# Two-layer graph block on one core: square root, reciprocal and shift of the normalising, once for both node groups of a step

## What is computed

```python
def conv(h, i):
    msg = h[src] * edge_weight[:, None]
    agg = jax.ops.segment_sum(msg, dst, num_segments=N)
    return agg @ W_rel[i] + b_rel[i] + h @ W_root[i]
# _layernorm: (x - m) / jnp.sqrt(v + eps), over the 128 features of a node
x = _layernorm(x + _L0_gnn_ref(x, edge_index, edge_weight, W_rel, b_rel, W_root))
x = _layernorm(x + _L1_gnn_ref(x, edge_index, edge_types, W, b))
```

## Time and profile before

| | |
|---|---|
| median of 3 runs | 1509.75 us (1504.82 to 1514.61) |
| the profiled execution | 1525.14 us, its span 1523.4 us |
| mean granted TensorE clock | 0.927 |
| busy share of the span | PE 81%, DVE 66%, POOL 55%, ACT 48% |
| layer 3, first to last residual add on DVE | 758 to 1075 us |
| last layer, first typed product to the end | 1097 to 1523 us |

### The profile page before, as it was taken

The page is one execution under the profiler, slowest core; times in us unless marked ns, Lnnn a source line. Parts: engine busy times, 40 slices in busy tenths (PEclk is TensorE's granted clock), DMA queues, the critical chain, the costliest instruction groups (busy, mean ns, idle before and its releaser), DMA issues.

```text
span 1523.4 us, 36509 instructions
## 1 busy us (share of the span) xinstructions
PE 1233.3 (81%) x6476; PEld 876.6 (58%) x6476; DVE 1000.5 (66%) x4006; ACT 729.2 (48%) x1674; POOL 831.9 (55%) x1154
## 2 busy tenths in 40 slices
PE   0599999999579997889378776778399999979984
PEld 0488888777457775667255554556145555445543
DVE  5566666565335554445289996878239999878886
ACT  0144443222124442212078886677326677756675
POOL 4776665561277775550577664650455666645520
PEclk9899999999889999999699998989669999998995
DMA  2599999999568888999599999999236666677775
GB/s 64 140 292 300 306 301 307 349 348 350 208 203 270 258 263 291 381 369 363 189 294 341 327 333 316 365 354 342 92 102 182 202 210 205 213 235 237 249 251 183
DMA packets 293061, 403.05 MB, mean 265 GB/s; under 512 B 43478, under 2 KB 202839, under 8 KB 292970
## 3 DMA queue, kind: packets, MB, share of 16 engines
q10 hardware_dynamic: 87120, 266.66, 47.3%
q1 hardware_dynamic: 180538, 83.67, 20.4%
q0 software_dynamic: 25312, 51.78, 12.8%
HBM read 222.77 MB, written 179.16 MB: 264 GB/s over the span
## 4 chain that ended last, share of the span: by engine, by line
DMA 25%; PE 24%; issue 14%; DVE 13%; SPq 13%; ACT 5%; POOL 3%; ACTq 2%; DVEq 1%; POOLq 0%
DMA win<-edge_rows 7%; PE ps_node L1256 7%; DMA feat_t<-spill 6%; PE ps_node L1247 5%; SPq L542 5%; PE ps_pair L1279 5%; DMA win<-plain_rows 4%; DVE ln_stats L1030 4%; SPq L545 3%; SPq L534 3%; DMA edge_rows<-edge_out 3%; POOL gather_ring L649 3%; PE ps_pair L1224 2%; ACT rows L1466 2%; DMA plain_rows<-gather_ring 2%
## 5 line engine op out<-in xcount | busy, mean ns | idle before, releaser
L649 POOL DMA_INDIRECT gather_ring<-h,src_ring x588 | 563.9, 959 | 261.0 <-issue 148.1
L1256 PEld LDWEIGHTS ps_node<-place,win 128*128 128x128 f32 x1764 | 288.4, 196 | 235.3 <-issue 173.7
L1256 PE MATMUL ps_node<-place,win 128*128 128x171 f32 (+1 forms) x1764 | 321.6, 319 | 68.8 <-DMA win<-plain_rows 58.9
L1412 ACT ACTIVATE next_t<-ps_node,rel_bt 128x512 f32<-128x512 f32 x294 | 199.9, 680 | 256.3 <-PE ps_node L1256 214.5
L972 DVE TENSOR_SCALAR place<-iota_row,window_node,window_weight 128x171 f32<-128x171 f32 (+1 forms) x882 | 280.6, 373 | 0.2
L1011 DVE COPY rows<-ps_pair 128x512 f32<-128x512 f32 x196 | 135.3, 690 | 210.2 <-PE ps_pair L1279 201.4
L1247 PE MATMUL ps_node<-feat_t,root_w 128*128 128x512 f32 x380 | 206.7, 627 | 58.5 <-DMA feat_t<-spill 54.7
L1466 ACT ACTIVATE rows<-resid,ln_shift,ln_rstd 128x128 f32<-128x128 f32 x576 | 235.8, 481 | 22.1 <-issue 22.1
L649 POOL DMA_INDIRECT gather_ring<-in_x,src_ring x196 | 186.7, 952 | 71.9 <-issue 55.2
L1279 PE MATMUL ps_pair<-rel_w,next_t 128*128 128x128 f32 x1568 | 208.2, 276 | 4.3 <-ACT next_t L1412 4.3
L1279 PEld LDWEIGHTS ps_pair<-rel_w,next_t 128*128 128x128 f32 x1568 | 197.6, 192 | 5.5 <-ACT next_t L1412 5.4
(11 more groups left out here) (115 smaller groups left out, 1164.0 us busy)
## 6 DMA issues: line engine op xcount, KB each, us to landing
h<-rows ACTq DMA_DIRECT2D x121, 512.0 KB
win<-plain_rows SPq DMA_DIRECT2D x588, 64.0 KB
edge_rows<-edge_out ACTq DMA_DIRECT2D x98, 264.0 KB
feat_t<-in_x_t ACTq DMA_DIRECT2D x49, 512.0 KB
plain_rows<-gather_ring ACTq DMA_DIRECT2D x98, 256.0 KB
resid<-in_x ACTq DMA_DIRECT2D x49, 512.0 KB
out_x<-rows ACTq DMA_DIRECT2D x49, 512.0 KB
spill<-next_t ACTq DMA_DIRECT2D x46, 512.0 KB
```

Of the source, the lines that this page charges most:

```text
L649: pool.indirect_dma_start(out=gather_ring[:, k.slot(4), j, 0:D], out_offset=None, in_=h_tabs[l][:, :], in_offset=bass.IndirectOffsetOnAxis ...
L1256: op = pe.matmul(bank[:, lo:hi], rows_j[:, 0:D], place_j, start=False, stop=(j == kind.count - 1))
L1412: act.activation(next_t[:, g.slot(4), :], ps_node[b][:, :], func, bias=rel_bt[:, l:l + 1]).then_inc(s_next, 1)
```

## The change

In layer 3 and in the last, `deviation`, `inverse_deviation` and `shift` take a step and not a group, and work on both its groups at once (128x8 and not 128x4). They are called in half 0 alone, for step m-2, that is for groups 2m-4 and 2m-3. In layer 3 the reciprocal stands right behind rows_out and the shift behind placement, both ahead of statistics. `normalise` still runs in each half on g-4, and now waits for the shift of its step. The rings of four groups are the same ones.

```diff
-                def inverse_deviation(l, g):
+                def inverse_deviation(l, m):
-                    dve.wait_ge(s_lnstd, (l - LAYERS + 1) * NGP + g.n + 1)
-                    dve.reciprocal(ln_rstd[:, g.slot(4), :], ln_std[:, g.slot(4), :]).then_inc(s_rstd, 1)
+                    both = slice(2 * m.slot(2), 2 * m.slot(2) + 2)
+                    dve.wait_ge(s_lnstd, (l - LAYERS + 1) * STEPS + m.n + 1)
+                    dve.reciprocal(ln_rstd[:, both, :], ln_std[:, both, :]).then_inc(s_rstd, 1)
-                def shift(l, g):
+                def shift(l, m):
-                    dve.wait_ge(s_rstd, q + 1)
+                    dve.wait_ge(s_rstd, (l - LAYERS + 1) * STEPS + m.n + 1)
+                    dve.scalar_tensor_tensor(out=ln_shift[:, both, :], in0=ln_mv[:, both, :, 0], scalar=-1.0,
+                                             in1=ln_rstd[:, both, :], op0=ALU.mult, op1=ALU.mult).then_inc(s_shift, 1)
 # DVE, layer 3
                                 rows_out(l, g.plus(-2))
+                                if not b:
+                                    inverse_deviation(l, m.plus(-2))
                                 placement(l, g.plus(1))
+                                if not b:
+                                    shift(l, m.plus(-2))
                                 statistics(l, g.plus(-2))
-                                inverse_deviation(l, g.plus(-3))
                                 moments(l, g.plus(-2))
-                                shift(l, g.plus(-3))
 # DVE, last layer
-                            inverse_deviation(l, g.plus(-3))
+                            if not b:
+                                inverse_deviation(l, m.plus(-2))
                             placement(l, g.plus(1))
-                            shift(l, g.plus(-3))
+                            if not b:
+                                shift(l, m.plus(-2))
 # ACT
-                def deviation(l, g):
+                def deviation(l, m):
+                    act.wait_ge(s_var, (l - LAYERS + 1) * NGP + 2 * m.n + 2)
+                    act.activation(ln_std[:, both, :], ln_mv[:, both, :, 1], ACT.Sqrt,
+                                   bias=eps_col[:, 0:1]).then_inc(s_lnstd, 1)
                 def normalise(l, g):
-                    act.wait_ge(s_shift, q + 1)
+                    act.wait_ge(s_shift, (l - LAYERS + 1) * STEPS + m.n + 1)
 # ACT, each step
-                            deviation(l, g.plus(-3))
+                            if not b:
+                                deviation(l, m.plus(-2))
```

More of the change, by code:

```diff
@@ L1042, in moments @@
                     op.then_inc(s_var, 1)
-                def inverse_deviation(l, g):
-                    if g.outside(NGP):
+                def inverse_deviation(l, m):
+                    if m.outside(STEPS):
                         return
-                    dve.wait_ge(s_lnstd, (l - LAYERS + 1) * NGP + g.n + 1)
-                    dve.reciprocal(ln_rstd[:, g.slot(4), :], ln_std[:, g.slot(4), :]).then_inc(s_rstd, 1)
-                def shift(l, g):
-                    if g.outside(NGP):
-                        return
-                    q = (l - LAYERS + 1) * NGP + g.n
-                    b = g.slot(4)
-                    dve.wait_ge(s_rstd, q + 1)
-                    dve.scalar_tensor_tensor(out=ln_shift[:, b, :], in0=ln_mv[:, b, :, 0], scalar=-1.0,
-                                             in1=ln_rstd[:, b, :], op0=ALU.mult, op1=ALU.mult).then_inc(s_shift, 1)
+                    both = slice(2 * m.slot(2), 2 * m.slot(2) + 2)
+                    dve.wait_ge(s_lnstd, (l - LAYERS + 1) * STEPS + m.n + 1)
+                    dve.reciprocal(ln_rstd[:, both, :], ln_std[:, both, :]).then_inc(s_rstd, 1)
+                def shift(l, m):
+                    if m.outside(STEPS):
+                        return
+                    both = slice(2 * m.slot(2), 2 * m.slot(2) + 2)
+                    dve.wait_ge(s_rstd, (l - LAYERS + 1) * STEPS + m.n + 1)
+                    dve.scalar_tensor_tensor(out=ln_shift[:, both, :], in0=ln_mv[:, both, :, 0], scalar=-1.0,
+                                             in1=ln_rstd[:, both, :], op0=ALU.mult, op1=ALU.mult).then_inc(s_shift, 1)
                 def residual(g):
@@ L1441, in load_residual @@
                                  ).then_inc(s_resid[m.slot(4)], 16)
-                def deviation(l, g):
-                    if l < LAYERS - 1 or g.outside(NGP):
+                def deviation(l, m):
+                    if l < LAYERS - 1 or m.outside(STEPS):
                         return
-                    q = (l - LAYERS + 1) * NGP + g.n
-                    act.wait_ge(s_var, q + 1)
-                    act.activation(ln_std[:, g.slot(4), :], ln_mv[:, g.slot(4), :, 1], ACT.Sqrt,
+                    both = slice(2 * m.slot(2), 2 * m.slot(2) + 2)
+                    act.wait_ge(s_var, (l - LAYERS + 1) * NGP + 2 * m.n + 2)
+                    act.activation(ln_std[:, both, :], ln_mv[:, both, :, 1], ACT.Sqrt,
                                    bias=eps_col[:, 0:1]).then_inc(s_lnstd, 1)
```

## The result

The changed kernel took 1540.93 us (median of 4 runs, 1531.27 to 1545.42) beside 1511.18 us for the kernel before (median of 4 runs): 1.0207 times as long, 95% interval 1.0154 to 1.026, or 30 us more. Run again later it took 1537.35 beside 1518.05 us, ratio 1.0122 (1.006 to 1.0185), 19 us more. The forecast was +27 us. All ratios here compare executions in the faster of the two states that executions of this kernel fall into, and need not equal the quotient of the medians.

What follows compares the result with a forecast made beforehand. DVE sets the pace in the last layer's first stretch, a loop through memory in its second; 8 + 14 + 4 + 1 = +27 us on the median of 1509.75 gives 1537 us, range 1504 to 1558.

Steps and rivals of the forecast that it cites:

- Last layer, first regime: Last layer's early steps, paced by DVE: delayed edge write exceeds its cover, 0.33 us a step over about 24 steps, +8 us.
- Reader to write: Last layer's memory loop, window's reader to the edge_rows write it releases: +2.0 us per two steps early, +1.50 later.
- the slack: Last layer, first regime: time from the last window's landing to its reader, 1.4 us, covering part of the delay.
- Last layer, second regime: Last layer's later steps, paced by the loop through memory: no slack, +0.75 us a step over 19 steps, +14 us.
- Write to reader: Last layer's memory loop, edge_rows write to the windows' reader; second regime has no slack, so +1.50 us per two steps remains.
- Layer 3, first stretch: Layer 3's steps bound by a one-step ring: +0.3 us a step over some 20 steps, partly swallowed by DMA waits, +4 us.
- The ring: Layer 3: root, reciprocal, placements, shift, normalise to the next root, one step long; 5.97 us against 5.66.
- DVE's gain: Reciprocal and shift saved on DVE: 0.16 us a step in the last layer, hidden in its first regime; 0 in layer 3.
- Rival B: Grouping in full: DVE and ACT give back whole instruction lengths, 30 us, to 1480 us; chance 0.03.
- Rival D: PE's half 1 products wait for scale_rows and hold take_grade back 0.5 us a step: +22 more, 1559 us; chance 0.08.
- Layer 3, second stretch: Layer 3's later steps: feature and residual loads stay ahead of normalise in ACT's queue, their start does not move, 0 us.
- The +1 for the two layer ends: At two layer ends normalise now waits for root, reciprocal and shift: +1 us.

Runs made afterwards that it cites:

- after_edges_first: Changed kernel, but in half 0 of the last layer ACT scales and writes the edges ahead of normalise; ratio to the kernel before 1.0082.
- before_again: The kernel before, unchanged, run again for a second trace; ratio 1.0002 to the kernel before.
- after_again: The changed kernel, unchanged, run again for a second trace; ratio 1.0122 to the kernel before.
- shift_early_edges_first: Changed kernel with an early square root before layer 3's walk, last layer's edges ahead of normalise, layer 3's shift ahead of placement; ratio 1.0045 to the kernel before.
- after_warm: Changed kernel plus one single-column square root on ACT ahead of the walk of layer 3; ratio 1.011 to the kernel before.

## Why the prediction was right

The sum, +27, held because an overestimate and an underestimate met; the path was right, the agreement of the number is in part luck. Term by term:

- *Last layer, first regime: +8, right.* Reader to write was to grow by 2.17 - 0.16 = 2.0 us and grew by 2.19; +0.33 us a step was forecast, +0.25 to 0.28 measured, in five traces. The size came out by two errors: the slack covered 1.2 us, near the 1.4 assumed, but the last window's flight shortened by 0.7 us where the prediction had flights 0.2 to 0.3 us longer. after_edges_first shows the cause by taking it away.
- *Last layer, second regime: +14, about twice too much.* The size of the wait was right: reader to write grew by 1.49 (5.93 to 7.42; 5.67 to 7.32 in the second pair) where +1.50 was forecast. The step that failed is the silent one after it, that the flights stay as they are. Write to reader shrank from 10.64 to 9.40 (10.33 to 9.27), so +0.75 us a step became +0.18 and +0.32 in the two pairs. At like clocks (0.97 for before_again, after and after_again) it is 0.32 to 0.46, 6 to 9 us over 19 steps. Chain of the kernel after, as the earlier trace rows:

```profile
1395.97 2.69 DMA edge_rows<-edge_out
1401.55 3.50 DMA win<-edge_rows
1405.20 0.06 DVE rel_dst L947
...
1412.47 2.90 DMA edge_rows<-edge_out
1418.18 3.84 DMA win<-edge_rows
```

A window flies 3.50 and 3.84 us here, 4.62 in the earlier trace rows; the write 2.69 and 2.90, 3.01 before. The opposite case is after_edges_first, with 5.39 and 11.89 us: 0.5 us won on one side of this loop against before, and 1.25 lost on the other. The prediction held the flights of one pair of steps for constants.
- *Layer 3, first stretch: +4, measured +12, the term that failed most.* The ring was found, with 5.97 us; it is 6.28. Ahead of normalise it takes 1.86 us and not 1.53: to the reciprocal 0.33, to placement 0.14 (0.09 assumed), to the shift 1.00 (0.91), to normalise 0.39 (0.18). From 6.02 to 6.29, without the table loads, is +6 us over 23 steps. The other 6 us are five of the six table loads (the sixth lies ahead of the stretch), of which the prediction has no word: it counted the roots that the change removes and did not ask where the first one now stands.
- *DVE's gain.* 0.09 + 0.07 us a step was near: where the edges stand ahead of the wait, it shows as 7.46 to 7.35, 7.33, 7.34 and 7.29, that is 0.11 to 0.17. Rival B, that whole lengths (0.31 us) are given back, falls.
- *Rival D, PE joins in, fell.* PE did wait for scale_rows, as the page of the kernel after has it:

```profile
L1228 PE MATMUL ps_pair<-typed_w,edge_t 128*128 128x384 f32 x392 | 181.0, 545 | 22.8 <-ACT edge_out L1380 22.1
```

Before, that group had an idle time of 0.0. But these 22.1 us were PE's own slack: DVE's take_grade behind it waited 1.1 us in the whole second stretch and not at all in the first.
- *Layer 3, second stretch, 0.* 6.70 and 6.79 before, 6.53 and 6.64 after, both within what the kernels with an unchanged layer 3 scatter here (6.40 to 6.79). The +1 for the two layer ends was not measured apart.
- *What no term had: the clock.* PE runs at the lower of its two levels for a while as the last layer starts, after a pause: in the kernel before it is busy 0 of 9 us from 1075 us on, at a mean clock of 0.66, and 1.55 of the 13 us behind that, at 0.50. From 1110 to 1130 us the kernel before is still there and the kernel after is not:

```profile
1110.00:1130.00 20.00, 20.00 (x38) 7.17 (x37) 4.29 (x10) 4.32 (x12) 11.16 (x20) 0.52 0.32 90
```

```profile
1110.00:1130.00 20.00, 17.93 (x63) 7.50 (x62) 8.81 (x21) 6.79 (x19) 15.85 (x25) 0.99 0.45 131
```

The mean over the whole start was 0.62 to 0.72 in the five kernels whose last layer is ungrouped, 0.69 to 0.81 in the nine whose last layer is grouped. The stretch took 79 to 90 us in the first (mean 84.5) and 73 to 82 in the second (mean 75.2). Stretches from layer 3's last residual add, kernel before:

```profile
1075.15:1159.74 84.59, 62.21 (x193) 28.80 (x193) 30.84 (x115) 25.29 (x70) 47.34 (x75) 0.68 0.33 99
```

and kernel after:

```profile
1083.00:1157.21 74.21, 51.18 (x192) 25.67 (x192) 30.77 (x109) 23.84 (x65) 46.10 (x75) 0.79 0.37 111
```

The same matmuls (one record fewer) took 62.21 us of PE at 0.68 and 51.18 at 0.79. If this is an effect of the change, it gave about 9 us back; the two ranges overlap, and no run tested it. It stays open.

The terms as measured, 12 + 6.5 + 6 to 9, are 25 to 28 us; with the 9 us at the start of the last layer given back, 15 to 18. The two comparisons of medians say 30 us (23 to 39 by the interval) and 19 us (9 to 28). The profiled executions themselves are only 6.1 us apart (spans 1523.4 and 1529.5) and 13.6 (1529.0 and 1542.6). In both pairs the start of the last layer is 10 to 14 us shorter in the changed kernel, and the rest of layer 3 is 4.5 us shorter, which is in its scatter. So the stretches carry the forecast's terms one by one, but they don't add up to the 30 us of the first comparison; what lies between stays open.

## What to carry over

Before two small operations are merged into one, look for who used the first result early, and for what stands behind that user in its queue: here 0.16 us a step on DVE was bought with 2.2 us of delay for a DMA issue that merely stood behind the wait, and moving the issue ahead of the wait took the loss out of that stretch. Check too whether the merged operation still runs once before a hardware loop: here it did not, and the load of ACT's table moved into the loop and was paid for each turn. And in a loop that passes through memory, take the compute part from the trace but give the flights a range: write to reader shrank by 1.1 to 1.2 us when the issue came 1.5 to 1.65 us later, and grew by 1.25 us when it came 0.5 us earlier.

## What the runs showed of the hardware

- An ACT_TABLE_LOAD takes 1.283 us in every one of these traces, and the one that stood in a hardware loop was executed in each of its six turns, though one load served them all in after_warm.
- The last window of a table write (57.8 KB) flew 2.6 us in the first stretch of the last layer and 4.0 us in the second in the kernel before, the write (264 KB) 2.5 and 3.9 us. In the second stretch both were shorter where the write was issued later (2.9 and 3.65 us in the kernel after) and longer where it was issued earlier (4.35 and 4.6 us in shift_early_edges_first).
- A reciprocal of 128x8 takes 198 ns against 164 ns for 128x4, the shift 159 against 144, the root 301 against 295: doubling the width costs 6 to 34 ns.
- The granted TensorE clock of one stretch of unchanged code differed between 0.83 and 0.97 from trace to trace, and with it the stretch by 18 us. In the second stretch of the last layer the kernels that write their edges late had 0.95 to 0.99 (six traces), those that write them early 0.83 to 0.97 (eight traces). PE has gaps there in either; why the clock falls more often in one was not found.
